# Output projection of an attention and LSTM kernel: one float32 matmul replaced by three float16 ones, with high and low parts made by three engines

## The chip, the cores and the metric

The kernel runs on one core of a Trainium2 chip. The metric is the device time of one execution, in microseconds. A core has TensorE (PE, matmuls; its weight loads are listed as PEld), VectorE (DVE), ScalarE (ACT), GpSimd (POOL) and SyncE (SP), whose queue issues most of the DMAs.

## The reference, cut to what matters

```python
x = x + attn(layernorm(x))          # x: 32 batches x 256 rows x 128
x = x + lstm(layernorm(x))          # 32 steps, one per batch
# attn: h = rms_norm(x); q, k, v = split(h @ w_qkv.T); rope(q), rope(k)
#       16 heads of 64; 4 extra keys and values in front; causal softmax
#       out = softmax(q k^T / 8) v   (256 x 1024 per batch)
#       return out @ w_out.T         # the output projection, 1024 -> 128
```

## The kernel before

Five instruction streams are written out by hand, one per engine; each engine works in order, and semaphores tie the engines together. The streams run over iterations j = 0 to 34 and in each over eight slots s = 0 to 7, one for each pair of heads. In an iteration, batch j is projected to queries and keys and rotated (slot s handles pair s), batch j-1 goes through scores, exponentials and values, batch j-2 is normalised and put through the output projection, and batch j-3 does its step of the LSTM (called gates and state). So four batches are in flight, and a full iteration is 8 slots of PE work.

The path that the prediction follows, for one iteration:

- `invert(j-2)` on DVE at the end of slot 1 takes the reciprocal of the softmax sums of batch j-2 (line 832, tile `linv`).
- SP stores it to DRAM (`store_linv`, line 301) and then spreads it over the partitions into `rinv` (`spread_linv`, line 312, four DMAs of 256 KB). Its place in SP's queue is slot 2, after `swap(j, 2)` and so ahead of `swap(j, 3)`.
- `swap(j, s)` (line 294) moves the partition-swapped half of the rotation, `rope_b` to `rope_c`. `rotate(j, s)` on DVE (lines 798 and 799) writes `rope_a` and `rope_b`; since `rope_b` has two buffers, `rotate(j, 5)` waits until the swap of pair 3 has landed. `rope_add` on POOL (line 407) adds the two to `qk`, and ACT's `hi` (line 529) makes the float16 copy `qk_h`.
- `divide` on DVE (line 845) multiplies two pairs of `raw`, the attention output of batch j-2, by `rinv`: parts n = 0 and 1 in slot 4, n = 2 and 3 in slot 5. A part n holds the pairs 2n and 2n+1.
- `project_out` on PE (line 1179) multiplies a part with `wo_sb` in float32, four matmuls of 128x128x128 per part; parts 0 and 1 in slot 5, parts 2 and 3 in slot 6. A float32 matmul shows as two instructions in the profile.
- `residual` (line 850) and `second_stats` on DVE in slot 6, `rstd` on POOL and `second_norm` on ACT in slot 7, `transpose_xn` and the gates on PE in slots 0 to 2 of the next iteration.

Between these stand, in each slot, `project` (line 1034) at the slot's start on PE, `scores_for_max` (line 1073), `scores_t` (line 1098) and `attend` (line 1142), in some slots `values` (lines 1053 and 1056) and `sums` (line 1163); on DVE `rotate` and four `maxima` (line 809); on POOL `prob_add` (line 400); on ACT `exp`, `raw_copy` and `hi`. In slots 3 and 7 PE begins with `transpose_top` (line 1081), which waits for all `maxima` of four pairs. `h_low` on DVE (line 742) in slot 5 makes the low part of the next batch's input. `project(s)` waits until DVE has read the bank of `project(s-1)`.

The other projections are already done in two float16 parts each: `SPLIT` lists the three products high x high, high x low, low x high.

## Time and profile before

| | us |
|---|---|
| median of 3 runs | 1133.13 |
| lowest and highest of them | 1126.74 to 1135.27 |
| profiled execution, its own time | 1133.03 |
| span of its trace | 1131.2 |

The span runs from the first to the last instruction in the trace; the time of the profiled execution is 1.8 us longer. An iteration shows in the trace as the distance of one `linv` instruction to the next. In the rows, a time in brackets at the end is how long the engine sat idle before the instruction, and what released it.

### The profile page before, as it was taken

To read this page: it belongs to the slowest core of one execution; us is meant where nothing else is said; L and a number is where in the kernel's file an instruction comes from. 1 tells how busy PE (TensorE), PEld (TensorE's weight loads), DVE (VectorE), ACT (ScalarE), POOL (GpSimd) and SP (SyncE) were. 2 spreads that over 40 slices of the span, in tenths; PEclk is the share of its full clock that TensorE was granted. 3 is DMA by queue.
4 is the path that set the end of the run, shared out by engine and by line. 5 is a ranking of instruction groups with operands and counts; after the bars stand their busy time and mean duration, and the time that the engine had idled before them with its cause. 6 is when DMAs were issued, how large, how long until landed. Compare 5 with 4: busy or idle time off the path is not lost.

```text
span 1131.2 us, 47261 instructions
## 1 busy us (share of the span) xinstructions
PE 1080.3 (95%) x18443; PEld 813.6 (72%) x18443; DVE 930.0 (82%) x3305; ACT 698.4 (62%) x1575; POOL 634.8 (56%) x816
## 2 busy tenths in 40 slices
...
DMA packets 78031, 120.52 MB, mean 107 GB/s; under 512 B 13041, under 2 KB 35954, under 8 KB 77682
## 3 DMA queue, kind: packets, MB, share of 16 engines
...
## 4 chain that ended last, share of the span: by engine, by line
PE 59%; DVE 16%; DMA 14%; SPq 4%; issue 3%; POOL 2%; ACT 1%; DVEq 0%; POOLq 0%
PE bank_pv L1142 11%; PE bank L1034 11%; DMA rope_c<-rope_b 10%; PE bank_st L1098 8%; PE bank_sum L1179 5%; PE bank_sum L1163 4%; DVE masked L809 4%; PE bank_sm L1073 4%; PE bank L1056 3%; DMA linv_scratch<-linv 3%; SPq L312 3%; DVE linv L832 2%; DVE rope_a L798 2%; PE bank L1281 2%; PE bank L1283 2%
## 5 line engine op out<-in xcount | busy, mean ns | idle before, releaser
L407 POOL TENSOR_TENSOR qk<-rope_a,rope_c 128x512 f32<-128x512 f32 x256 | 341.0, 1332 | 312.9 <-DMA rope_c<-rope_b 288.9
L809 DVE CUSTOM_DVE_ANT_0 masked<-bank_sm,mask_q 128x132 bf16<-128x132 f32 (+1 forms) x1024 | 307.1, 355 | 17.7 <-PE bank_sm L1073 17.2
L798 DVE TENSOR_TENSOR rope_a<-bank,cos 128x512 f32<-128x512 f32 x256 | 174.1, 680 | 130.1 <-PE bank L1034 83.7
L400 POOL TENSOR_TENSOR prob<-prob 128x264 f32<-128x264 f32 x256 | 210.8, 823 | 117.1 <-ACT prob L544 108.3
L529 ACT ACTIVATE qk_h<-qk 128x512 f16<-128x512 f32 x256 | 160.4, 627 | 172.2 <-POOL qk L407 171.7
L544 ACT ACTIVATE prob<-bank_st 128x784 f32<-128x784 f32 x256 | 209.3, 817 | 59.7 <-PE bank_st L1107 58.9
L1142 PE MATMUL bank_pv<-prob,v_sb 128*64 128x256 f32 (+1 forms) x2048 | 224.8, 340 | 0.6 <-DVE raw L825 0.6
L1098 PE MATMUL bank_st<-qk 64*64 64x256 f32 (+3 forms) x4096 | 186.3, 299 | 0.4 <-issue 0.2
L1098 PEld LDWEIGHTS bank_st<-qk 64*64 64x64 f32 x4096 | 167.7, 134 | 9.6 <-issue 1.3
L799 DVE TENSOR_TENSOR rope_b<-bank,sin 128x512 f32<-128x512 f32 x256 | 173.8, 679 | 0.0
L1142 PEld LDWEIGHTS bank_pv<-prob,v_sb 128*64 128x64 f32 x2048 | 124.3, 136 | 54.4 <-issue 0.9
L1034 PE MATMUL bank<-h_hi,w_hi 128*128 128x256 f16 x512 | 143.5, 280 | 5.8 <-DVE rope_b L799 5.0
L1034 PE MATMUL bank<-h_hi,w_lo 128*128 128x256 f16 x512 | 141.8, 277 | 0.0
L1034 PE MATMUL bank<-h_lo,w_hi 128*128 128x256 f16 x512 | 141.6, 277 | 0.0
L1179 PE MATMUL bank_sum<-wo_sb,raw 128*128 128x128 f32 x992 | 122.7, 276 | 0.0
L1179 PEld LDWEIGHTS bank_sum<-wo_sb,raw 128*128 128x128 f32 x992 | 116.0, 192 | 1.9 <-DVE raw L845 1.1
L578 ACT ACTIVATE v_sb<-bank 128x512 f32<-128x512 f32 x128 | 75.8, 593 | 48.2 <-PE bank L1053 28.7
L569 ACT ACTIVATE raw<-bank_pv 128x256 f32<-128x256 f32 x256 | 97.7, 382 | 4.1 <-PE bank_pv L1148 3.1
L845 DVE SCALAR_TENSOR_TENSOR raw<-rinv,raw 128x512 f32<-128x512 f32 x124 | 96.6, 819 | 2.0 <-DMA rinv<-linv_scratch 1.8
L1073 PEld LDWEIGHTS bank_sm<-qk_h 64*64 64x64 f16 x2048 | 37.6, 105 | 82.7 <-issue 56.6
L1073 PE MATMUL bank_sm<-qk_h 64*64 64x68 f16 (+3 forms) x2048 | 86.7, 246 | 4.4 <-ACT qk_h L529 3.1
L809 DVE DVE_READ_ACCUMULATOR2_ANT top<- 128x1 bf16 x1024 | 85.7, 84 | 0.1
...
## 6 DMA issues: line engine op xcount, KB each, us to landing
rope_c<-rope_b SPq DMA_DIRECT2D x512, 128.0 KB, 2.3
...
v_end<-v_end_scratch SPq DMA_DIRECT2D x64, 8.0 KB
v_sb<-pm_v SPq DMA_DIRECT2D x63, 8.0 KB
```

Of the source, the lines that this page charges most:

```text
L400: G.tensor_tensor(prob_2[:, s % 4, :, :], prob[:, s % 4, :, 0:NT - Q1], prob[:, s % 4, :, C0 + Q1:SCOL], ALU.add).then_inc(S["prob_added"], 1)
L407: G.tensor_tensor(qk[:, s, :].rearrange("p (u n) -> p u n", u=2)[:, :, 0:NT], rope_a[:, (NPAIR * j + s) % 3, :].rearrange("p (u n) -> p u ...
L529: A.activation(qk_h[:, s, :].rearrange("p (u n) -> p u n", u=2)[:, :, 0:NT], qk[:, s, :].rearrange("p (u n) -> p u n", u=2)[:, :, 0:NT], A ...
L544: A.activation(prob[:, s % 4, :, :], ps_st[:, :, 0:SCOL], ACT.Exp).then_inc(S["exp_done"], 1)
L798: V.tensor_tensor(rope_a[:, (NPAIR * j + s) % 3, :], proj_bank(j, s)[:, :], cos[:, :], ALU.mult)
L799: V.tensor_tensor(rope_b[:, s % 2, :], proj_bank(j, s)[:, :], sin[:, :], ALU.mult).then_inc(S["qk_read"], 1)
L809: ins = V.tensor_tensor_reduce(masked[:, e, c0:c0 + n], ps_sm[:, e, c0:c0 + n], mask_q[:, c0:c0 + n], 1.0, LOWEST, ALU.add, ALU.max, top[: ...
L1034: last = T.matmul(proj_bank(j, s)[:, u * NT:(u + 1) * NT], W[q][:, col:col + P], H[p][:, par, NPM:NKEY], start=(i == 0), stop=(i == 2))
L1073: last = T.matmul(ps_sm[OWN[SIDE[qb]], e, c0:c0 + n], qk_h[OWN[e], s, qb * HB:qb * HB + HB], qk_h[OWN[e], s, NT:NT + n], start=True, stop= ...
L1098: T.matmul(ps_st[OWN[SIDE[kb]], e, st_cols(blk)], qk[OWN[e], s, NT + kb * HB:NT + kb * HB + HB], qk[OWN[e], s, q0:NT], start=(kc == 0), st ...
L1142: last = T.matmul(ps_pv[OWN[e], q0:NT], v_sb[:, kc, col:col + DH], prob[:, s % 4, e, c0:c0 + NT - q0], start=(kc == 0), stop=(kc == 1))
L1179: last = T.matmul(y_out(cj)[:, q * D:(q + 1) * D], raw[:, par, s, q * P:(q + 1) * P], wo_sb[:, s, :], start=(alone and s == 0 and q == 0), ...
```

## The change

The output projection is done as the others are. `w_out` is loaded into a raw area and cast to `wo_hi` and `wo_lo` (scale 64, once, at the start; `residual` divides by 64 again). For each part, ACT casts the normalised `raw` to float16 (`y_high`, into `y_hl`), and the difference is the low part (`y_low`): parts 0 and 2 (pairs 0, 1, 4, 5) by DVE (`y_low_dve`), parts 1 and 3 by POOL. PE does three float16 matmuls for each float32 one. The last two batches are split otherwise: the last but one gets all its low parts from POOL, the last from DVE.

`y_hl` lies in the same memory as `rinv`, so a `rinv` of the next batch may be loaded only when the projection is done (`spread_linv` waits for `y_ready`). In the engines' orders, `project_out` of parts 0 and 1 moves from slot 5 to slot 6, parts 2 and 3 go from the front of slot 6 to its end; `residual` and `second_stats` move to slot 7, `rstd` behind a `rope_add`, `second_norm` to slot 0 of the next iteration, `xt_high` and `xt_low` to slot 1; `transpose_xn` and the gates go to the end of their slots on PE, and ACT's `gate_tanh` one slot later.

```diff
@@ -77,12 +77,14 @@
+        o_raw = pre_f[:, 3 * DI + 8 * P + NCONST:3 * DI + 8 * P + NCONST + DI]
...
-        wo_sb = sb("wo_sb", [P, NPAIR, D], f32)
+        wo_hi = sb("wo_hi", [P, NPAIR, D], f16)
+        wo_lo = sb("wo_lo", [P, NPAIR, D], f16)
@@ -138,7 +140,8 @@
-        rinv = sb("rinv", [P, NPAIR, NT], f32)
+        y_hl = sb("y_hl", [P, 4, 2, 2 * NT], f16)
+        rinv = y_hl[:, :, :, :].rearrange("p n u m -> p (n u m)").bitcast(f32).rearrange("p (s n) -> p s n", s=NPAIR)
@@ -304,7 +306,7 @@
-                wait(sp, S["norm_done"], 4 * cj)
+                wait(sp, S["y_ready"], cj)
@@ -409,6 +411,13 @@
+            def y_low(cj, par, n):
+
+                pool.wait_ge(S["y_hi_done"], 4 * cj + n + 1)
+                done = S["y_lo_pool" if cj < NB - 2 else "y_lo_done"]
+                G.tensor_tensor(y_hl[:, n, 1, :].rearrange("p (s n) -> p s n", s=2), raw[:, par, 2 * n:2 * n + 2, :],
+                                y_hl[:, n, 0, :].rearrange("p (s n) -> p s n", s=2), ALU.subtract).then_inc(done, 1)
+
             def rstd(cj):
@@ -432,14 +441,21 @@
-                    if c and s == 7 and j < NB:
-                        rstd(j - 2)
+                    if s == 6 and c and j < NB:
+                        y_low(j - 2, p, 3)
...
+                    if s == 5 and c and j < NB:
+                        y_low(j - 2, p, 1)
+                    if s == 7 and c and j < NB:
+                        rstd(j - 2)
...
+                    if s in (5, 6) and j == NB:
+                        y_low(j - 2, p, 2 * (s - 5))
+                        y_low(j - 2, p, 2 * (s - 5) + 1)
@@ -514,6 +531,8 @@
+                act.wait_ge(S["ld_wo"], 16)
+                cast(A.activation(wo_hi[:, :, :].rearrange("p c d -> p (c d)"), o_raw, ACT.Copy, scale=WS))
@@ -630,6 +649,12 @@
+            def y_high(cj, par, n):
+
+                act.wait_ge(S["norm_done"], 4 * cj + n + 1)
+                A.activation(y_hl[:, n, 0, :].rearrange("p (s n) -> p s n", s=2), raw[:, par, 2 * n:2 * n + 2, :],
+                             ACT.Copy).then_inc(S["y_hi_done"], 1)
+
@@ -638,18 +663,21 @@
-                    if s == 3 and b:
-                        copy_top(j - 1, 1)
...
-                    if s == 0 and d and j != NB + 1:
+                    if s == (0 if j > NB else 1) and d and j != NB + 1:
...
+                    if s == 1 and j == NB + 1:
+                        for n in range(4):
+                            y_high(j - 2, p, n)
...
-                    elif s in (1, 2) and d and j - 3 < NB - 1:
-                        gate_tanh(j - 3, s - 1)
+                    elif s in (2, 3) and d and j - 3 < NB - 1:
+                        gate_tanh(j - 3, s - 2)
+                    if s == 3 and b:
+                        copy_top(j - 1, 1)
@@ -657,14 +685,17 @@
+                    if s == 5 and c and j <= NB:
+                        y_high(j - 2, p, 0)
+                        y_high(j - 2, p, 1)
...
-                    if s == 7 and c and j < NB:
-                        second_norm(j - 2)
+                    if s == 0 and d and j <= NB:
+                        second_norm(j - 3)
@@ -689,6 +720,9 @@
+                    if s == 5 and c and j <= NB:
+                        y_high(j - 2, p, 2)
+                        y_high(j - 2, p, 3)
@@ -780,11 +814,14 @@
+                V.scalar_tensor_tensor(wo_lo[:, :, :].rearrange("p c d -> p (c d)"), o_raw, WS,
+                                       wo_hi[:, :, :].rearrange("p c d -> p (c d)"), ALU.mult,
@@ -844,10 +881,17 @@
+            def y_low_dve(cj, par, n):
+
+                dve.wait_ge(S["y_hi_done"], 4 * cj + n + 1)
+                V.tensor_tensor(y_hl[:, n, 1, :].rearrange("p (s n) -> p s n", s=2), raw[:, par, 2 * n:2 * n + 2, :],
+                                y_hl[:, n, 0, :].rearrange("p (s n) -> p s n", s=2), ALU.subtract).then_inc(S["y_lo_done"], 1)
+
...
-                V.tensor_tensor(at3(x_sb, cj), y_out(cj), at3(x_sb, cj), ALU.add).then_inc(S["x1_done"], 1)
+                V.scalar_tensor_tensor(at3(x_sb, cj), y_out(cj), 1.0 / WS, at3(x_sb, cj), ALU.mult,
+                                       ALU.add).then_inc(S["x1_done"], 1)
@@ -912,11 +956,13 @@
+                    if s == 7 and c and j < NB:
+                        residual(j - 2)
...
-                    if s == 0 and d and j != NB + 1:
+                    if s == (0 if j > NB else 1) and d and j != NB + 1:
@@ -924,9 +970,13 @@
+                    if s == 5 and c and j < NB:
+                        y_low_dve(j - 2, p, 0)
...
-                    if s == 6 and c:
+                    if s == 6 and c and j < NB:
+                        y_low_dve(j - 2, p, 2)
+                    if s == 6 and c and j >= NB:
@@ -941,6 +991,9 @@
+                            if i > 0:
+                                y_low_dve(j - 2, p, i - 1)
+                        y_low_dve(j - 2, p, 3)
@@ -952,7 +1005,7 @@
-                    if s == 6 and c:
+                    if s == (6 if j >= NB else 7) and c:
@@ -1172,13 +1225,20 @@
-                pe.wait_ge(S["norm_done"], 4 * cj + n + 1)
+                if cj < NB - 2:
+                    pe.wait_ge(S["y_lo_pool" if n % 2 else "y_lo_done"], 2 * cj + n // 2 + 1)
+                else:
+                    pe.wait_ge(S["y_lo_done"], 2 * (NB - 2) + 4 * (cj - NB + 2) + n + 1)
+                if cj == 0 and n == 0:
+                    pe.wait_ge(S["casts_dve"], 7)
...
-                        last = T.matmul(y_out(cj)[:, q * D:(q + 1) * D], raw[:, par, s, q * P:(q + 1) * P], wo_sb[:, s, :],
-                                        start=(alone and s == 0 and q == 0), stop=(s == NPAIR - 1 and q == QT - 1),
-                                        skip_group_check=True)
+                        at = s % 2 * NT + q * P
+                        for i, (u, v) in enumerate(SPLIT):
+                            last = T.matmul(y_out(cj)[:, q * D:(q + 1) * D], y_hl[:, n, u, at:at + P], WO[v][:, s, :],
+                                            start=(alone and s == 0 and q == 0 and i == 0),
+                                            stop=(s == NPAIR - 1 and q == QT - 1 and i == 2), skip_group_check=True)
@@ -1308,10 +1368,6 @@
-                    elif s == 0 and d and j <= NB:
-                        transpose_xn(j, j - 3)
-                    if s in (1, 2) and d and j <= NB:
-                        gates(j, j - 3, s - 1)
@@ -1327,7 +1383,10 @@
-                    if s in (5, 6) and c and j != NB:
+                    if s == 6 and c and j < NB:
+                        project_out(j - 2, p, 0)
+                        project_out(j - 2, p, 1)
+                    if s in (5, 6) and j == NB + 1:
@@ -1354,10 +1413,15 @@
+                    if s == 6 and c and j < NB:
+                        project_out(j - 2, p, 2)
+                        project_out(j - 2, p, 3)
...
-                if isinstance(j, int) and j == 2:
-                    pe.wait_ge(S["casts_dve"], 6)
+                    if s == 0 and d and j <= NB:
+                        transpose_xn(j, j - 3)
+                    if s in (1, 2) and d and j <= NB:
+                        gates(j, j - 3, s - 1)
```

GpSimd's queue from slot 4 to slot 7 of one iteration. The line with `qk` is `rope_add` (L407 before, L409 after), the one with `prob` is `prob_add`; the first row of each piece is the `rope_add` of pair 3. Before:

```order
L407 TENSOR_TENSOR qk<-rope_a,rope_c 128x2x256 [waits swapped1,st_ready]
L400 TENSOR_TENSOR prob<-prob 128x264 [waits exp_done,sum_ready]
L407 TENSOR_TENSOR qk<-rope_a,rope_c 128x2x256 [waits swapped0,st_ready]
L400 TENSOR_TENSOR prob<-prob 128x264 [waits exp_done,sum_ready]
L407 TENSOR_TENSOR qk<-rope_a,rope_c 128x2x256 [waits swapped1,st_ready]
```

After:

```order
L409 TENSOR_TENSOR qk<-rope_a,rope_c 128x2x256 [waits swapped1,st_ready]
L402 TENSOR_TENSOR prob<-prob 128x264 [waits exp_done,sum_ready]
L409 TENSOR_TENSOR qk<-rope_a,rope_c 128x2x256 [waits swapped0,st_ready]
L418 TENSOR_TENSOR y_hl<-raw,y_hl 128x512 [waits y_hi_done]
L402 TENSOR_TENSOR prob<-prob 128x264 [waits exp_done,sum_ready]
L418 TENSOR_TENSOR y_hl<-raw,y_hl 128x512 [waits y_hi_done]
L409 TENSOR_TENSOR qk<-rope_a,rope_c 128x2x256 [waits swapped1,st_ready]
```

The low part of part 1 stands behind the `rope_add` of pairs 3 and 4, that of part 3 ahead of the `rope_add` of pair 5.

PE's queue in slot 6, from its `project` on (L1034 before, L1088 after). Before:

```order
L1034 MATMUL bank<-h_lo,w_hi 128x256
L1179 MATMUL bank_sum<-wo_sb,raw 128x128 [waits norm_done]
L1179 MATMUL bank_sum<-wo_sb,raw 128x128 x3
...
L1053 MATMUL bank<-w_hi,h_hi 128x512 [waits h_lo_done]
...
L1073 MATMUL bank_sm<-qk_h 64x68 [waits max_done,hi_done]
...
L1081 MATMUL bank_sm<-ident_b,top 128x128 [waits max_done]
```

After:

```order
L1088 MATMUL bank<-h_lo,w_hi 128x256
L1239 MATMUL bank_sum<-wo_hi,y_hl 128x128 [waits y_lo_done]
...
L1239 MATMUL bank_sum<-wo_hi,y_hl 128x128 [waits y_lo_pool]
...
L1107 MATMUL bank<-w_hi,h_hi 128x512 [waits h_lo_done]
...
L1127 MATMUL bank_sm<-qk_h 64x68 [waits max_done,hi_done]
...
L1239 MATMUL bank_sum<-wo_hi,y_hl 128x128 [waits y_lo_done]
...
L1135 MATMUL bank_sm<-ident_b,top 128x128 [waits max_done]
```

Parts 0 and 1 now stand ahead of `values`, parts 2 and 3 at the end of the slot, and the second and fourth part wait for GpSimd (`y_lo_pool`).

DVE's queue from slot 5 to slot 6, without the `maxima` rows. Before:

```order
L799 TENSOR_TENSOR rope_b<-bank,sin 128x512
L845 SCALAR_TENSOR_TENSOR raw<-rinv,raw 128x512 [waits spread1]
L845 SCALAR_TENSOR_TENSOR raw<-rinv,raw 128x512
L742 SCALAR_TENSOR_TENSOR h_lo<-bank,nw,h_hi 128x256 [waits h_hi_done]
...
L798 TENSOR_TENSOR rope_a<-bank,cos 128x512 [waits swapped0,rope_sum,qk_proj]
...
L850 TENSOR_TENSOR x_sb<-bank_sum,x_sb 128x256 [waits y_ready]
```

After (`raw<-y_hl,raw` is `divide`, since `rinv` is a view of `y_hl`):

```order
L836 TENSOR_TENSOR rope_b<-bank,sin 128x512
L882 SCALAR_TENSOR_TENSOR raw<-y_hl,raw 128x512 [waits spread1]
L882 SCALAR_TENSOR_TENSOR raw<-y_hl,raw 128x512
L887 TENSOR_TENSOR y_hl<-raw,y_hl 128x512 [waits y_hi_done]
L776 SCALAR_TENSOR_TENSOR h_lo<-bank,nw,h_hi 128x256 [waits h_hi_done]
...
L835 TENSOR_TENSOR rope_a<-bank,cos 128x512 [waits swapped0,rope_sum,qk_proj]
...
L887 TENSOR_TENSOR y_hl<-raw,y_hl 128x512 [waits y_hi_done]
```

One low part comes in behind the divisions of slot 5, one behind the rotation of slot 6, and `residual` leaves slot 6.

## Rows read from the trace of the kernel before

**Rows 1.** The page's head and its first part: busy time of each engine.

```profile
span 1131.2 us, 47261 instructions
PE 1080.3 (95%) x18443; PEld 813.6 (72%) x18443; DVE 930.0 (82%) x3305; ACT 698.4 (62%) x1575; POOL 634.8 (56%) x816
```

**Rows 2.** Stretches: length, busy us of PE, PEld, DVE, ACT, POOL; clock; DMA share, GB/s.

```profile
413.60:446.20 32.60, 30.74 (x540) 23.24 (x538) 27.19 (x94) 19.02 (x43) 17.79 (x22) 1.00 0.36 101
```

**Rows 3.** Timeline of DVE: start, length, line, what; several iterations.

```profile
80.30 1.75 DVE L832 RECIPROCAL linv<-bank_sum 128x256 f32<-128x256 f32 x1
...
408.79 1.75 DVE L832 RECIPROCAL linv<-bank_sum 128x256 f32<-128x256 f32 x1
...
424.91 0.69 DVE L798 TENSOR_TENSOR rope_a<-bank,cos 128x512 f32<-128x512 f32 x1 [2.98 <-DMA rope_c<-rope_b]
...
443.76 1.75 DVE L832 RECIPROCAL linv<-bank_sum 128x256 f32<-128x256 f32 x1
...
509.08 1.75 DVE L832 RECIPROCAL linv<-bank_sum 128x256 f32<-128x256 f32 x1
...
519.91 1.29 DVE L845 SCALAR_TENSOR_TENSOR raw<-rinv,raw 128x512 f32<-128x512 f32 x2
...
522.77 0.69 DVE L798 TENSOR_TENSOR rope_a<-bank,cos 128x512 f32<-128x512 f32 x1 [1.24 <-DMA rope_c<-rope_b]
...
523.98 1.84 DVE L845 SCALAR_TENSOR_TENSOR raw<-rinv,raw 128x512 f32<-128x512 f32 x2
525.74 0.47 DVE L742 SCALAR_TENSOR_TENSOR h_lo<-bank,nw,h_hi 128x256 f16<-128x256 f32 x1
...
540.50 0.30 DVE L809 CUSTOM_DVE_ANT_0 masked<-bank_sm,mask_q 128x132 bf16<-128x132 f32 x1 [0.36 <-PE bank_sm L1073]
...
541.63 1.75 DVE L832 RECIPROCAL linv<-bank_sum 128x256 f32<-128x256 f32 x1
...
1037.35 1.75 DVE L832 RECIPROCAL linv<-bank_sum 128x256 f32<-128x256 f32 x1
```

**Rows 4.** Timeline of SP: the spreading of `rinv`, and the swap of pair 3 behind it.

```profile
513.70 2.40 SPq L312 DMA_DIRECT2D rinv<-linv_scratch  x4
516.28 2.19 SPq L294 DMA_DIRECT2D rope_c<-rope_b  x2
```

**Rows 5.** Timeline of PE, slots 5 and 6 of the same iteration.

```profile
520.57 0.28 PE L1034 MATMUL bank<-h_hi,w_hi 128*128 128x256 f16 x1
...
521.45 1.95 PE L1179 MATMUL bank_sum<-wo_sb,raw 128*128 128x128 f32 x16
...
525.16 0.28 PE L1034 MATMUL bank<-h_hi,w_hi 128*128 128x256 f16 x1
...
525.83 1.95 PE L1179 MATMUL bank_sum<-wo_sb,raw 128*128 128x128 f32 x16
527.62 0.38 PE L1053 MATMUL bank<-w_hi,h_hi 128*128 128x512 f16 x1
...
530.18 0.28 PE L1081 MATMUL bank_sm<-ident_b,top 128*128 128x128 bf16 x2
```

**Rows 6.** Timeline of PE near the end: float16 matmuls 128x128, back to back.

```profile
1100.17 0.22 PE L1241 MATMUL bank_st<-f_hi,xt 128*128 128x128 f16 x1
...
1100.84 0.22 PE L1241 MATMUL bank_sm<-f_hi,xt 128*128 128x128 f16 x1
```

**Rows 7.** Timeline of POOL, slots 4 and 5 of the same iteration.

```profile
522.78 1.27 POOL L407 TENSOR_TENSOR qk<-rope_a,rope_c 128x512 f32<-128x512 f32 x1 [4.95 <-DMA rope_c<-rope_b]
524.02 1.25 POOL L400 TENSOR_TENSOR prob<-prob 128x264 f32<-128x264 f32 x1
525.23 1.71 POOL L407 TENSOR_TENSOR qk<-rope_a,rope_c 128x512 f32<-128x512 f32 x1
```

**Rows 8.** Timeline of ACT in slot 4, the copy of pair 3.

```profile
524.09 0.63 ACT L529 ACTIVATE qk_h<-qk 128x512 f16<-128x512 f32 x1 [3.48 <-POOL qk L407]
```

**Rows 9.** Waits of DVE over the span: us in total, times, longest.

```profile
DVE rope_a L798 <- DMA rope_c<-rope_b: 43.6, 31, 3.1
```

More of the change, by code:

```diff
@@ L172, in build @@
             "qk_proj qk_read swapped0 swapped1 rope_sum hi_done sm_ready max_done top_tr top_copied "
-            "st_ready exp_done prob_added pv_ready raw_done sum_ready linv_done linv_stored spread0 spread1 norm_done y_ready x1_done "
+            "st_ready exp_done prob_added pv_ready raw_done sum_ready linv_done linv_stored spread0 spread1 norm_done y_hi_done y_lo_done y_lo_pool y_ready x1_done "
             "v_ready v_done v_end sx_done sx_rstd xn_ready xt_ready xt_hi_done xt_lo_done gate_ready gate_read c_hi_done state_done "
```

13 lines of the change are left out of this document (7 added, 6 removed).

## The prediction

> **What bounds the kernel now.** Start with the page's busy times [rows 1]: TensorE is busy 95% of 1131.2 us, VectorE 82%, GpSimd 56%. That invites the reading "TensorE is the bound, a cheaper projection is a gain". It is half true. The next view is VectorE's timeline at the one instruction that stands once in each iteration, the reciprocal `linv` [rows 3]. From 509.08 to 541.63 an iteration takes 32.55 us, from 408.79 to 443.76 it takes 34.97 us with the same instructions. In the second one TensorE is busy 30.74 of 32.60 us, at the full granted clock of 1.00 [rows 2], so it waited. The first and the last of the 30 starts of full iterations (80.30 and 1037.35) give a mean of 957.05/29 = 33.00 us.
>
> What differs is a transfer. Behind `linv` SP stores it, spreads it (2.40 us of issue) and only then issues the swap of pair 3 [rows 4]. VectorE's `rotate` of slot 5 waits for that swap to land. This moment, called L below, is the start of that rope_a row. L is 522.77 - 509.08 = 13.69 us behind `linv` in the short iteration and 424.91 - 408.79 = 16.12 us in the long one. From L to the next `linv` it is 541.63 - 522.77 = 18.86 and 443.76 - 424.91 = 18.85 us [rows 3]. So two things end together: TensorE's own work, 32.55 us, and a loop through the DMAs, (time from `linv` to L) + 18.86. The loop has no slack left: each 0.1 us put between L and the next `linv` lengthens the iteration by about 0.1 us. The mean L is then 33.00 - 18.86 = 14.14 us behind `linv`. VectorE waited at this point 31 times, 43.6 us in all [rows 9]; here 1.24 us.
>
> The question for the change is therefore not what TensorE saves but what it puts behind L.
>
> **What TensorE saves.** Two parts in float32 take 527.62 - 525.83 = 1.79 us [rows 5]. Twelve float16 matmuls of 128x128 take 1100.84 - 1100.17 = 0.67 us, 56 ns each [rows 6]; the form of the operands is the same. A part now has 2 x 2 x 3 = 12, so two parts take 1.34 us. Saved: 0.45 us for two parts, 0.90 us for a batch, 28.8 us for 32 batches if nothing waits.
>
> **What stands between L and the end of slot 6 before.** Slot 7 begins with the `transpose_top` at 530.18, which is L + 7.41 [rows 5]. VectorE's rotation takes 1.21 us (522.77 to 523.98), the two divisions 1.76 (to 525.74) [rows 3], and TensorE reaches parts 2 and 3 at 525.83 [rows 5], 0.1 us later.
>
> **What stands there after.** Part by part, with L = 0:
>
> GpSimd: `rope_add` of pair 3 at 0.0, `prob_add` at 1.25, `rope_add` of pair 4 at 2.46, done at 526.94, which is 4.17 [rows 7]. These three were there before, but nobody on TensorE waited for them so soon. Now the low part of part 1 is queued behind them, though its data could be had earlier. Its price is not in the trace (float16 in and out). The nearest row is the `rope_add` with the same 128x512 elements and two inputs: 1.27 us alone, 1.71 us when VectorE's divisions run beside it [rows 7]. The upper bound is 1.9 us, the crowded one and a little for the conversion. From below I take 0.7, less than any row of half the size. I take 1.3, the lone one, since VectorE then reads PSUM in `h_low` and the maxima. The low part of part 0 on VectorE starts at 525.74, or 2.97, beside the `rope_add`, which I let lengthen by 0.2. Part 1 is ready at 4.17 + 0.2 + 1.3 = 5.7 (5.1 to 6.3).
>
> This crowding is a row: two divisions take 1.29 us at 519.91, with GpSimd idle, and 1.84 us at 523.98 with it busy [rows 3, 7]. The Trainium skill says so too (GPSIMD Engine Reference, Specifications): GpSimd's SBUF interface is shared with VectorE, and instructions of VectorE with two SBUF inputs contend. By that rule both new kinds of instruction crowd each other, and the trace agrees.
>
> The same page (Performance versus the Vector engine) speaks against the division of labour itself: elementwise work with two inputs costs GpSimd about 2.6 cycles an element, roughly double VectorE, and belongs on VectorE. By its figure the low part would be an estimate of 512 x 2.6 / 1.2 GHz = 1.1 us, which would make the sum 6 us smaller.
>
> ACT: its copy of pair 3 begins at 524.09 and takes 0.63 us [rows 8]. The high parts 0 and 1 are queued behind it, at 0.6 us each: done by L + 3.2. That is ahead of GpSimd's 4.4 and near VectorE's 2.97, so they decide nothing. The exponential of slot 5 is 1.2 us later; TensorE needs it only behind `values`.
>
> TensorE: the projection of slot 6 waits for the rotation, till 1.2, and ends at 1.9. Part 0 waits for VectorE's low part (2.97 + 0.6 to 0.9, so till 3.8) and ends at 4.5. Part 1 waits till 5.7 and ends at 6.4. `values`, scores and `attend` take 530.18 - 527.62 = 2.56 us [rows 5], to 8.95; the low parts of 2 and 3 are there by then (GpSimd: 5.7 + 0.8 + 1.3 to 1.7, so 8.2 at the latest). Parts 2 and 3 take 1.34 us: slot 7 begins at L + 10.3.
>
> That is 10.3 - 7.4 = 2.9 us later than before, with TensorE idle for about 3.9 us in slot 6.
>
> From slot 7 to the next `linv` I count no change. `residual` and `second_stats` (some 1.2 us of VectorE) come into slot 7, but VectorE has waited by then. The gates' move takes away a wait of 0.36 us ahead of the maxima of slot 1 (the row at 540.50 [rows 3]), and `xt_low` comes into the same slot at about the same price. The new wait of SP, `y_ready` of the batch before, was met an iteration's third earlier. Behind it stand `rinv`, all swaps, and so the rotations; it would matter only if the projection ran past slot 2. From `linv` to L I keep 14.14 us: the same queue, the same bytes.
>
> **The sum.** Iteration: 14.14 + 18.86 + 2.9 = 35.9 us, against 33.0. It holds in the 30 iterations in which the projection stands behind a swap: 30 x 2.9 = 87 us. The last two batches have no swaps; there the chain division, high part, low part is longer by a low part of 1.3 us on GpSimd and some 1.6 us at the very end, less 2 x 0.9 us in TensorE, and the start gets one more cast each on ACT and VectorE of about 1.2 us: together +3 us, an estimate. Span 1131.2 + 87 + 3 = 1221; the profiled execution was 1.8 us longer than its span, 1133.03, and the median 1133.13 is the same within 0.1. Forecast 1223 us. With the bounds of GpSimd's low part (-0.6 to +0.6 us, 30 times) it is 1205 to 1241.
>
> **Rivals.**
>
> *TensorE alone decides (faster).* If the swap landed early enough, or the low parts were ready when TensorE comes, the 28.8 us would be saved, less 3: 1107 us. For it: TensorE's 32.55 us is a floor hit in many iterations. Against: the 18.86 us repeat to 0.01 us in iterations 2.4 us apart in length. Even this needs L at least 2 us earlier. Chance 0.06.
>
> *Unchanged (within 1%).* GpSimd's part is hidden, so that an iteration loses 1.6 us as in the next rival, and L comes 1.3 to 1.9 us earlier because the transfers collide less: 1133 + 3 + 30 x (-0.3 to +0.3), 1127 to 1145 us. The spread of L, 13.69 to 16.12, shows that it moves by such amounts; against it, 13.69 would have to become 12.4 at the most. Chance 0.06.
>
> *VectorE's chain decides, not GpSimd (slower, less).* The place is slot 6, with GpSimd's low part ready before VectorE's. Then part 0 starts at 3.8, both end at 5.1, slot 7 begins at 5.1 + 2.56 + 1.34 = 9.0: +1.6 us an iteration, 1133 + 48 + 3 = 1184 us. It decides if the low part on GpSimd is done by 4.5; its queue is busy till 4.17, so that needs an operation of 0.3 us. A milder form is a GpSimd queue that drains faster once the longer iteration sets it free. Chance 0.15.
>
> *The wait grows past TensorE (slower, more).* The exponential of slot 5, 1.2 us later, and `rope_add` of pair 5 behind both low parts, could delay slots 6 to 0: another 0.5 to 1 us each time, 1240 to 1255 us. Chance 0.13.
>
> My case, GpSimd's low part of part 1 as the last to arrive: chance 0.60.
>
> A measurement of this kernel can tell about 1% from no change. Slower by over 1%: 0.60 + 0.15 + 0.13 = 0.88; within 1%: 0.06; faster: 0.06. The range, 8 in 10, takes in half of the milder rival and part of the heavier: 1178 to 1245 us.
>
> **What would show it.** Right: `linv` to `linv` near 35.9 us, L to the next `linv` near 21.8, a wait of TensorE in front of the projection that names GpSimd's `y_hl`, near 1.3 us each time, and one that names VectorE's, near 1.9; TensorE's busy share near 87%; the matmuls of a part 0.67 us. Wrong in size: GpSimd's `y_hl` far from 1.3 us, or L not 14.1 us behind `linv`. Wrong in mechanism: iterations below 33 us, or TensorE waiting elsewhere, at `transpose_top` or the exponential.

## The result, and the profile after

| | before | after |
|---|---|---|
| time, median | 1133.04 us (4 runs) | 1253.79 us (4 runs; 1253.48 to 1256.66) |
| ratio | | 1.108 (95%: 1.103 to 1.113) |
| profiled span | 1131.2 us | 1252.3 us |
| mean iteration, first to 30th `linv` | 33.00 us | 36.92 us |
| mean L, counted from `linv` | 14.15 us | 14.02 us |
| L to the next `linv` | 18.69 to 19.71 us, mean 18.85 | 21.72 to 23.34 us, mean 23.10 |

The last two rows are of the iterations in which VectorE waits for the swap: all 29 before, 21 of 29 after. Slower, as forecast, but by 120.8 us and not by 90; 1253.79 lies above the range's end of 1245. An iteration grew by 3.92 us instead of 2.9.

The page's head and its first part after the change, against [rows 1]:

```profile
span 1252.3 us, 48543 instructions
PE 1099.5 (88%) x18955; PEld 807.2 (64%) x18955; DVE 1015.7 (81%) x3370; ACT 760.8 (61%) x1704; POOL 723.9 (58%) x880
```

TensorE's projection got cheaper, and yet its busy time rose from 1080.3 to 1099.5 us. Work that costs less and sums to more is the first hint at what the forecast lacked: the same matmuls ran slower somewhere. VectorE's busy time rose by 86 us, though its 64 low parts would take 64 x 0.68 = 44 us at their shortest length.

Waits of TensorE over the span (us in total, times, longest):

```profile
PE bank_sum L1239 <- DVE y_hl L887: 76.6, 30, 3.1
PE bank_pv L1195 <- DVE raw L862: 16.5, 30, 0.6
PE bank L1088 <- DVE rope_b L836: 11.8, 20, 1.9
...
PE bank_sum L1239 <- POOL y_hl L418: 3.1, 18, 0.2
```

The place is the forecast one, in front of the projection. But the long wait is for VectorE's low part of part 0 (2.5 us each), and GpSimd's part 1 adds 0.2. The second row is new too: in slot 1 of the next iteration `attend` waits 0.55 us each time for VectorE's copy of `raw`; before, such waits sum to 0.6 us.

Two neighbouring iterations, VectorE's timeline. The rows are the reciprocals and the two rotations at L:

```profile
635.55 1.75 DVE L869 RECIPROCAL linv<-bank_sum 128x256 f32<-128x256 f32 x1
...
649.05 0.69 DVE L835 TENSOR_TENSOR rope_a<-bank,cos 128x512 f32<-128x512 f32 x1 [0.27 <-DMA rope_c<-rope_b]
...
672.35 1.75 DVE L869 RECIPROCAL linv<-bank_sum 128x256 f32<-128x256 f32 x1
...
685.71 0.69 DVE L835 TENSOR_TENSOR rope_a<-bank,cos 128x512 f32<-128x512 f32 x1 [0.47 <-DMA rope_c<-rope_b]
...
707.43 1.75 DVE L869 RECIPROCAL linv<-bank_sum 128x256 f32<-128x256 f32 x1
```

From L to the next `linv` the first takes 672.35 - 649.05 = 23.30 us, the second 707.43 - 685.71 = 21.72. The forecast was 18.86 + 2.9 = 21.76. The second is the forecast iteration; 24 of 29 are like the first.

TensorE's timeline tells the two apart. First iteration, then second:

```profile
653.82 0.23 PE L1239 MATMUL bank_sum<-wo_hi,y_hl 128*128 128x128 f16 x1 [2.51 <-DVE y_hl L887]
...
654.84 0.23 PE L1239 MATMUL bank_sum<-wo_hi,y_hl 128*128 128x128 f16 x1 [0.17 <-POOL y_hl L418]
...
655.53 0.63 PE L1107 MATMUL bank<-w_hi,h_hi 128*128 128x512 f16 x1
...
657.22 1.30 PE L1151 MATMUL bank_st<-qk 64*64 64x256 f32 x16
...
661.02 0.28 PE L1135 MATMUL bank_sm<-ident_b,top 128*128 128x128 bf16 x2
...
690.49 0.23 PE L1239 MATMUL bank_sum<-wo_hi,y_hl 128*128 128x128 f16 x1 [2.38 <-DVE y_hl L887]
...
692.18 0.38 PE L1107 MATMUL bank<-w_hi,h_hi 128*128 128x512 f16 x1
...
693.09 0.72 PE L1151 MATMUL bank_st<-qk 64*64 64x256 f32 x16
...
696.10 0.28 PE L1135 MATMUL bank_sm<-ident_b,top 128*128 128x128 bf16 x2
```

The projection's matmuls are alike, and the waits nearly (2.51 and 2.38 us). But the first `values` matmul lasts 0.63 us in one and 0.38 in the other, the scores 1.30 and 0.72. Slot 7 begins at L + 11.97 in the first and at L + 10.39 in the second; the forecast was 10.3. Stretches of 2 us, columns as in [rows 2], first iteration and then second:

```profile
652.00:654.00 2.00, 0.18 (x3) 0.18 (x4) 2.00 (x3) 2.00 (x6) 2.00 (x2) 1.00 0.21 75
654.00:656.00 2.00, 1.83 (x26) 1.38 (x24) 2.00 (x11) 1.25 (x3) 2.00 (x3) 0.88 0.01 4
656.00:658.00 2.00, 2.00 (x21) 1.06 (x23) 1.51 (x5) 0.60 (x1) 2.00 (x2) 0.50 0.09 34
658.00:660.00 2.00, 2.00 (x38) 1.53 (x31) 1.37 (x8) 1.04 (x2) 0.37 (x2) 0.77 0.32 110
...
690.00:692.00 2.00, 1.34 (x21) 1.18 (x22) 2.00 (x11) 1.91 (x5) 2.00 (x2) 1.00 0.03 8
692.00:694.00 2.00, 2.00 (x48) 1.35 (x45) 2.00 (x6) 0.60 (x1) 2.00 (x3) 1.00 0.00 0
```

Behind an idle stretch of 2.5 us the granted clock falls from 1.00 to 0.50, from 2.4 to 1.2 GHz, while TensorE has work, and comes back some 3.4 us later. What is lost is (0.12 + 0.50 + 0.23) x 2 = 1.7 us of TensorE's time; slot 7 shows 1.58 us of it. In the second iteration the clock stayed, behind 2.38 us. Over the trace, the five iterations that keep the full clock have idle stretches of 2.02 to 2.38 us in front of the projection, and of the 24 in which it falls 23 have 2.51 us or more; but one of them has 2.21 us, so the length of this stretch does not decide alone.

Last, why VectorE's low part came late. Timelines of VectorE and of GpSimd, same slot:

```profile
650.26 1.83 DVE L882 SCALAR_TENSOR_TENSOR raw<-y_hl,raw 128x512 f32<-128x512 f32 x2
652.02 1.75 DVE L887 TENSOR_TENSOR y_hl<-raw,y_hl 128x512 f16<-128x512 f32 x1
...
656.41 0.75 DVE L887 TENSOR_TENSOR y_hl<-raw,y_hl 128x512 f16<-128x512 f32 x1
```

```profile
651.51 1.71 POOL L409 TENSOR_TENSOR qk<-rope_a,rope_c 128x512 f32<-128x512 f32 x1
653.18 1.61 POOL L418 TENSOR_TENSOR y_hl<-raw,y_hl 128x512 f16<-128x512 f32 x1
...
655.45 1.15 POOL L418 TENSOR_TENSOR y_hl<-raw,y_hl 128x512 f16<-128x512 f32 x1
```

The low part (L887) begins beside GpSimd's `rope_add` and lasts 1.75 us. It ends at 653.77, 0.55 us behind the `rope_add`'s end of 653.22: it seems to have done its work only then. Of the 64 low parts of VectorE 34 last 0.68 to 0.75 us and 26 last 1.75; only four lie between.

### The profile page after: what moved, and what is told of

It is laid out like the page before. It is cut to its first block, busy times and chain, and to the rows that moved or that the text cites. A ratio compares the mean times of both kernels' runs of the same rounds, so it can differ in the third digit from the quotient of the medians.

```text
span 1252.3 us, 48543 instructions
## 1 busy us (share of the span) xinstructions
PE 1099.5 (88%) x18955; PEld 807.2 (64%) x18955; DVE 1015.7 (81%) x3370; ACT 760.8 (61%) x1704; POOL 723.9 (58%) x880
## 4 chain that ended last, share of the span: by engine, by line
PE 38%; DMA 19%; DVE 18%; POOL 9%; SPq 7%; issue 6%; ACT 1%; DVEq 0%; POOLq 0%; ACTq 0%
DMA rope_c<-rope_b 13%; PE bank_sum L1239 8%; PE bank_pv L1195 6%; DMA linv_scratch<-linv 6%; PE bank L1088 5%; SPq L314 5%; POOL qk L409 4%; PE bank_st L1151 4%; DVE linv L869 4%; DVE masked L846 3%; PE bank L1107 3%; PE bank_sum L1216 3%; POOL y_hl L418 3%; PE bank_sm L1127 2%; PE bank L1110 2%
## 5 line engine op out<-in xcount | busy, mean ns | idle before, releaser
L409 POOL TENSOR_TENSOR qk<-rope_a,rope_c 128x512 f32<-128x512 f32 x256 | 351.3, 1372 | 263.8 <-DMA rope_c<-rope_b 254.1
L846 DVE CUSTOM_DVE_ANT_0 masked<-bank_sm,mask_q 128x132 bf16<-128x132 f32 (+1 forms) x1024 | 307.0, 355 | 25.3 <-PE bank_sm L1127 25.2
L1195 PE MATMUL bank_pv<-prob,v_sb 128*64 128x256 f32 (+1 forms) x2048 | 224.7, 340 | 19.0 <-DVE raw L862 16.5
L1151 PE MATMUL bank_st<-qk 64*64 64x256 f32 (+3 forms) x4096 | 190.8, 304 | 1.1 <-ACT prob L563 1.1
L1239 PE MATMUL bank_sum<-wo_hi,y_hl 128*128 128x128 f16 x992 | 114.4, 240 | 79.8 <-DVE y_hl L887 76.6
L1151 PEld LDWEIGHTS bank_st<-qk 64*64 64x64 f32 x4096 | 172.6, 138 | 11.0 <-ACT prob L563 1.5
L1195 PEld LDWEIGHTS bank_pv<-prob,v_sb 128*64 128x64 f32 x2048 | 127.5, 136 | 72.3 <-issue 23.8
L1088 PE MATMUL bank<-h_hi,w_hi 128*128 128x256 f16 x512 | 142.9, 279 | 12.9 <-DVE rope_b L836 11.8
L1239 PEld LDWEIGHTS bank_sum<-wo_hi,y_hl 128*128 128x128 f16 x992 | 87.8, 108 | 97.4 <-DVE y_hl L887 85.0
L1088 PE MATMUL bank<-h_hi,w_lo 128*128 128x256 f16 x512 | 141.9, 277 | 0.0
L1088 PE MATMUL bank<-h_lo,w_hi 128*128 128x256 f16 x512 | 141.5, 276 | 0.0
L1239 PE MATMUL bank_sum<-wo_lo,y_hl 128*128 128x128 f16 x496 | 102.2, 240 | 0.0
L882 DVE SCALAR_TENSOR_TENSOR raw<-y_hl,raw 128x512 f32<-128x512 f32 x124 | 101.7, 860 | 0.3 <-DMA y_hl<-linv_scratch 0.3
```

The lines of the kernel that those rows point to most:

```text
L409: G.tensor_tensor(qk[:, s, :].rearrange("p (u n) -> p u n", u=2)[:, :, 0:NT], rope_a[:, (NPAIR * j + s) % 3, :].rearrange("p (u n) -> p u ...
L846: ins = V.tensor_tensor_reduce(masked[:, e, c0:c0 + n], ps_sm[:, e, c0:c0 + n], mask_q[:, c0:c0 + n], 1.0, LOWEST, ALU.add, ALU.max, top[: ...
L1088: last = T.matmul(proj_bank(j, s)[:, u * NT:(u + 1) * NT], W[q][:, col:col + P], H[p][:, par, NPM:NKEY], start=(i == 0), stop=(i == 2))
L1151: T.matmul(ps_st[OWN[SIDE[kb]], e, st_cols(blk)], qk[OWN[e], s, NT + kb * HB:NT + kb * HB + HB], qk[OWN[e], s, q0:NT], start=(kc == 0), st ...
L1195: last = T.matmul(ps_pv[OWN[e], q0:NT], v_sb[:, kc, col:col + DH], prob[:, s % 4, e, c0:c0 + NT - q0], start=(kc == 0), stop=(kc == 1))
L1239: last = T.matmul(y_out(cj)[:, q * D:(q + 1) * D], y_hl[:, n, u, at:at + P], WO[v][:, s, :], start=(alone and s == 0 and q == 0 and i == 0 ...
```

## The experiments

The theory after the two traces had three terms on top of [rows 3]'s 18.86 us: the moved projection, the wait for the parts, and the fall of the clock. The rivals said that the loop through L explains less than that, and that the part instructions cost whatever their place. All ratios are to the kernel before, measured beside each run.

### Keep TensorE busy while it waits

40 float16 matmuls of zeros are added to the projection's accumulation in front of the first wait, so the result is the same.

```
+    if cj < NB - 2 and n == 0:
+        for _ in range(40):
+            T.matmul(y_out(cj)[:, 0:P], w_hi[:, 0:P], zz[:, :], start=False, stop=False, ...)
     if cj < NB - 2:
         pe.wait_ge(S["y_lo_pool" if n % 2 else "y_lo_done"], 2 * cj + n // 2 + 1)
```

> The changed kernel with 40 float16 matmuls of 128x128 with a zero operand put ahead of the wait for the first low part in slot 6 (40 x 56 ns = 2.24 us, inside the wait of 2.5 to 2.6 us). Theory 'the clock is the missing term' (L to the next linv is 21.7 us in the iterations at clock 1.00 and 23.0 to 23.3 us in those at 0.95): granted clock 1.00 everywhere, L to linv 21.6 to 22.0 us in all iterations, time 1253.8 - 30 x 1.25 = 1216 us (1208 to 1226). Rival 'the low part on VectorE, 1.75 us instead of the 0.6 to 0.9 forecast, lengthens the loop': the filled wait changes nothing, 1250 to 1260 us. If the filler runs past the wait, iterations get longer than after.

Measured: 1213.0 us (1212.1 to 1213.9), ratio 1.072 (1.067 to 1.077), as expected. In the 13 iterations of 29 in which VectorE waits for the swap it is now 21.72 to 21.74 us from L to `linv`; the mean iteration is 35.47 us, the clock 1.00 in all 29, and the span's clock 0.988 instead of 0.955. Rows of one iteration, and its stretch behind the projection:

```profile
346.94 0.23 PE L1244 MATMUL bank_sum<-wo_hi,y_hl 128*128 128x128 f16 x1 [0.37 <-DVE y_hl L889]
...
348.64 0.38 PE L1109 MATMUL bank<-w_hi,h_hi 128*128 128x512 f16 x1
```

```profile
348.00:350.00 2.00, 2.00 (x37) 1.43 (x40) 2.00 (x7) 0.87 (x3) 2.00 (x3) 1.00 0.00 0
```

1200 matmuls more make the kernel 41 us faster, though VectorE's low part still ends at the same place behind L. That is the clock's term, shown: it is what the forecast lacked.

The other 16 iterations do not hang on L: the swap has landed, or all but landed, when VectorE comes to the rotation. In nine of them that costs nothing (34.86 to 35.09 us). In six the landing is so early that GpSimd's `rope_add` starts beside the state's instruction `c`, which then lasts 1.49 us instead of 0.42; these six take 36.07 us.

### The new order with the old projection

The changed kernel's order with float32 weights and matmuls from `raw`, and no high and low parts.

```
-    for i, (u, v) in enumerate(SPLIT):
-        last = T.matmul(..., y_hl[:, n, u, at:at + P], WO[v][:, s, :], ...)
+    last = T.matmul(..., raw[:, par, s, q * P:(q + 1) * P], wo_sb[:, s, :], ...)
```

> The changed kernel's order of work with the old float32 projection straight from raw: no high or low parts at all. Theory (loop through the DMAs): the order alone puts 1.2 + 0.67 + 1.79 + 2.56 + 1.79 = 8.05 us between L and slot 7 against 7.41 before, so 33.6 us an iteration, 1133 + 30 x 0.64 = 1152 us (1145 to 1160), no wait of TensorE at the projection, clock 1.00. Rival 'the moved order is the cause, not the parts': above 1200 us. Rival 'TensorE's own work decides': 1133 us.

Measured: 1157.9 us, ratio 1.024 (1.020 to 1.028), within the range expected. From L to `linv` it is 19.75 us, 0.9 more than the mean before, and TensorE waits at no projection. The ten shortest iterations take 33.17 us, 0.62 more than TensorE's own 32.55 before; 0.55 us is the wait at `attend`, which this run has too (16.5 us in all). The iterations give the decomposition: before 33.00, new order 33.82, with the parts and a full clock 35.47, with the clock's fall 36.92. Order 0.8, parts 1.65, clock 1.45 us; times 30 it is 25, 50 and 44 us. About 0.1 us of the order's 0.8 is one iteration of 37.01 us, in which the clock fell behind another idle stretch, of 2.14 us in front of `project`.

### All low parts on VectorE

```
-    pool: y_low(j - 2, p, 1) in slot 5, y_low(j - 2, p, 3) in slot 6
+    dve:  y_low_dve(j - 2, p, 1) in slot 5, y_low_dve(j - 2, p, 3) in slot 6
```

> The changed kernel with all four low parts by VectorE (part 1 in slot 5, part 3 in slot 6), none by GpSimd. Theory (VectorE's instruction with two inputs and GpSimd's instructions exclude each other, so that work moved from one to the other still queues): low part 0 ends at L + 4.75 us as now, low part 1 at about L + 6.05 instead of 5.8, slot 7 0.3 to 0.9 us later, 1265 us (1250 to 1285). Rival (GpSimd's own slower low parts, 1.2 to 1.6 us against 0.7 on VectorE, hold up the projection): faster by 30 us or more, 1225 or less.

Measured: 1254.6 us, ratio 1.110 (1.107 to 1.114), the changed kernel's time, and within the range expected. TensorE starts part 0 at L + 4.77 in every iteration in which VectorE waits for the swap, part 1 at L + 5.92 to 6.03. So taking the subtraction from GpSimd gains nothing: GpSimd's slower instruction, which the forecast took for the last to arrive, is not the cause. VectorE's own timeline of this run:

```profile
611.91 1.83 DVE L878 SCALAR_TENSOR_TENSOR raw<-y_hl,raw 128x512 f32<-128x512 f32 x2
613.66 2.90 DVE L883 TENSOR_TENSOR y_hl<-raw,y_hl 128x512 f16<-128x512 f32 x2
```

Two low parts take 2.90 us, where two alone take 1.3. This run also has an iteration that keeps the full clock behind an idle stretch as long as those behind which it falls:

```profile
988.27 0.23 PE L1234 MATMUL bank_sum<-wo_hi,y_hl 128*128 128x128 f16 x1 [2.59 <-DVE y_hl L883]
```

```profile
990.00:992.00 2.00, 1.88 (x44) 1.24 (x41) 2.00 (x8) 0.60 (x1) 0.50 (x1) 1.00 0.00 0
```

### What VectorE and GpSimd do to each other, by itself

Six phases behind the last store of the kernel before, on scratch tiles of 128x512 float32: 8 instructions of VectorE, 5 of GpSimd, each phase begun together. In the first two one of the engines does only 128x8 copies.

```
+    dve:  (0, 2, 5) tensor_tensor(sbuf, sbuf)   (3) tensor_tensor(psum, sbuf)   (4) tensor_copy(sbuf)
+    pool: (1, 2, 3, 4) tensor_tensor(sbuf, sbuf)   (5) tensor_copy(sbuf)
```

> The kernel before with six phases appended behind the last store, on scratch tiles, 128x512 float32 each: (0) 8 VectorE additions of two SBUF tiles alone, (1) 5 GpSimd additions alone, (2) both together, (3) VectorE's with one input from PSUM beside GpSimd's, (4) VectorE copies (one SBUF input) beside GpSimd's additions, (5) VectorE's additions of two SBUF tiles beside GpSimd copies. Exclusion theory: alone 0.6 us and 1.25 us an instruction; in phase 2 an instruction of VectorE ends about 0.55 us behind one of GpSimd's, so 1.7 to 1.9 us while GpSimd runs, and GpSimd's grow too; in phase 3 both keep their lengths. Phases 4 and 5 tell which inputs matter; by the float32 copies and conversions seen beside GpSimd so far I expect no loss in 4 and a loss in 5. Rival (a shared bandwidth, both slowed in proportion): in phase 2 VectorE about 0.9 us each, evenly.

Measured, timeline of VectorE, then of GpSimd (rows of one kind are grouped, the length is from the first's start to the last's end):

```profile
1129.44 4.91 DVE L1009 TENSOR_TENSOR raw<-rope_a 128x512 f32<-128x512 f32 x8 [5.13 <-DMA out<-x_sb]
...
1140.75 10.23 DVE L1009 TENSOR_TENSOR raw<-rope_a 128x512 f32<-128x512 f32 x8 [1.28 <-POOL qk L457]
1151.11 4.88 DVE L1011 TENSOR_TENSOR raw<-bank_pv,rope_a 128x512 f32<-128x512 f32 x8
1157.36 8.10 DVE L1013 COPY raw<-rope_a 128x512 f32<-128x512 f32 x8 [1.37 <-POOL qk L457]
1165.59 7.00 DVE L1009 TENSOR_TENSOR raw<-rope_a 128x512 f32<-128x512 f32 x8
```

```profile
1134.49 6.17 POOL L457 TENSOR_TENSOR qk<-rope_b 128x512 f32<-128x512 f32 x5 [1.90 <-DVE raw L1009]
1140.83 8.40 POOL L457 TENSOR_TENSOR qk<-rope_b 128x512 f32<-128x512 f32 x5 [0.17 <-POOL qk L457]
1151.11 6.16 POOL L457 TENSOR_TENSOR qk<-rope_b 128x512 f32<-128x512 f32 x5 [1.89 <-DVE raw L1009]
1157.44 7.07 POOL L457 TENSOR_TENSOR qk<-rope_b 128x512 f32<-128x512 f32 x5 [0.17 <-POOL qk L457]
1165.58 4.67 POOL L459 COPY qk<-rope_b 128x512 f32<-128x512 f32 x5 [1.08 <-DVE raw L1013]
```

Alone, 4.91 and 6.17 us; together 10.23, almost the sum of 11.08. Within it VectorE's instructions last 1.74 us each while GpSimd works, against 0.68 behind it and 0.69 alone, as in the kernel; GpSimd's last 1.70 us, against 1.26. With one input from PSUM (1151.11) neither loses anything. The rival, a shared bandwidth that slows all evenly, would give VectorE a single length. I missed phase 4: a plain float32 copy of one SBUF tile and GpSimd's addition exclude each other too, 1.48 us a piece against 0.41 behind it. The Trainium skill has both (SBUF — State Buffer, "SBUF: two separate sides"): the port pair that VectorE and GpSimd share is an exclusive lock for a whole instruction, taken by an instruction of GpSimd, or by one of VectorE with two SBUF inputs or in a two-port mode, and a float32 copy within SBUF is its example of that mode. The runs agree on which instructions block; the lengths are from the runs.

### Move the parts ahead of L

High parts 0 and 1 in slot 4 in front of pair 3's copy, low part 0 at the end of slot 4, low part 1 in front of GpSimd's `rope_add(3)`, high parts 2 and 3 in slot 5.

```
 act   y_high(0), y_high(1): s == 5 -> s == 4     y_high(2), y_high(3): ahead of hi() in s == 5
 dve   y_low_dve(0): s == 5 -> end of s == 4
 pool  y_low(1): ahead of rope_add(3)             y_low(3): behind rope_add(4)
```

> The changed kernel with the high and low parts 0 and 1 taken ahead of the landing of pair 3's swap (high parts 0, 1 by ScalarE in slot 4, low part 0 by VectorE at the end of slot 4, low part 1 by GpSimd ahead of rope_add(3)), high parts 2, 3 in slot 5 ahead of hi(4), low part 3 behind rope_add(4). Loop theory (the loss is the loop from the landing of pair 3's swap through division, high part, low part, projection, top of slot 7, back to the reciprocal): what follows that landing shrinks from 11.7 us to about 8.6 us, the period from 36.9 to about 33.9 us, TensorE's idle time at the projection becomes too short for its clock to fall, and the time is about 1160 us (1150 to 1180). Rival (the 16 high and low part instructions of an iteration cost what they cost on VectorE, GpSimd and ScalarE wherever they stand): 1230 us or more.

Measured: 1178.9 us, ratio 1.044 (1.041 to 1.046), within the range expected; 19 of 29 iterations take 34.35 to 34.38 us (mean 34.38), against 33.9 expected. This takes back 75 of the 121 us with the same instructions, so place decides and the second theory falls. Some 41 of the 75 us are the clock's, as in the run with filler: it stays at 1.00 in all 29 iterations here. What bounds it now is VectorE:

```profile
747.34 0.69 DVE L887 TENSOR_TENSOR y_hl<-raw,y_hl 128x512 f16<-128x512 f32 x1
747.94 0.69 DVE L835 TENSOR_TENSOR rope_a<-bank,cos 128x512 f32<-128x512 f32 x1
748.54 0.68 DVE L836 TENSOR_TENSOR rope_b<-bank,sin 128x512 f32<-128x512 f32 x1
749.14 2.84 DVE L882 SCALAR_TENSOR_TENSOR raw<-y_hl,raw 128x512 f32<-128x512 f32 x2
```

The rotation at 747.94 waits for no swap, as in most iterations of this run. Divisions 2 and 3 take 2.84 us beside GpSimd, against 1.29 for 0 and 1. In each stretch of 2 us from 740 to 760 VectorE is busy for 2.00, so its own chain is the bound here, and TensorE waits 0.97 us for its `h_low`, 0.39 for its maxima and 0.34 for its low part 2.

### All divisions and high parts ahead of L

As above, and divisions 2 and 3 in slot 4, all high parts in slot 4, half of the projection at the end of slot 5.

```
-    if s == 5 and c and j - 2 < NB - 1:   (dve)
-        divide(j - 2, p, 2); divide(j - 2, p, 3)
+        y_low_dve(j - 2, p, 0); divide(j - 2, p, 2); divide(j - 2, p, 3)      (dve, s == 4)
```

> The order of the early run, and also: divisions 2, 3 in slot 4, in the time in which VectorE waits for pair 3's swap, all four high parts in slot 4, the projection's halves at the ends of slots 5 and 6 instead of both in slot 6. Theory (loop from that landing): what follows the landing is about 6.5 us, the loop's period about 31.9 us, near TensorE's own busy time of an iteration of about 31.6 us, so about 1100 us (1095 to 1125), faster than the kernel before. Rival (VectorE's and GpSimd's mutual exclusion gives it back, as with the spread in halves): 1133 us or more.

Measured: 1205.3 us, ratio 1.067 (1.064 to 1.069). A clear miss: 34.62 us or more an iteration instead of 31.9, 26 us slower than the milder version. The state's instruction `c` now fell beside a `rope_add`, and the rotation of slot 5 behind it. TensorE's `project` of slot 6 waits for that rotation, some 2.1 us in most iterations:

```profile
PE bank L1087 <- DVE rope_b L836: 63.3, 34, 2.4
```

In eight of 29 iterations the clock falls behind this wait, and they take 36.0 to 36.7 us; those at full clock take 34.62 to 35.38. Timeline of VectorE in this run, and then in the next:

```profile
623.23 1.49 DVE L948 SCALAR_TENSOR_TENSOR c<-ga,gb 128x256 f32<-128x256 f32 x1
...
628.56 0.68 DVE L887 TENSOR_TENSOR y_hl<-raw,y_hl 128x512 f16<-128x512 f32 x1
```

### The same, with c ahead of the divisions

```
+    if s == 4 and d and j != NB + 1: state(j - 3, 1)        # now ahead of divide(0..3)
```

> The same move of c in the run that has all four divisions, all high parts and low part 0 in slot 4 (1205 us, iteration 34.6 us, VectorE without a pause between slots 3 and 7). Theory (VectorE's own chain there, in which two-input instructions queue with GpSimd's, sets the iteration): c 0.35 instead of 1.4 us, iteration 33.6 us, 1172 us (1160 to 1185), still slower than the kernel before. Rival (the projection or the landing of the swaps sets it): 1205 us, no change.

Measured: 1214.6 us, ratio 1.075 (1.072 to 1.078): slower still.

```profile
698.79 0.42 DVE L948 SCALAR_TENSOR_TENSOR c<-ga,gb 128x256 f32<-128x256 f32 x1
...
708.28 1.75 DVE L887 TENSOR_TENSOR y_hl<-raw,y_hl 128x512 f16<-128x512 f32 x1
```

`c` fell from 1.49 to 0.42 us as expected, and slot 5's rotation came 1.07 us earlier. But low part 2 in slot 6 began 0.07 us behind a `rope_add` of GpSimd instead of 0.21 us ahead of one, and went from 0.68 to 1.75 us. What was gained in slot 4 was lost in slot 6, 1.07 us each, and TensorE got a wait for that low part (25.3 us in all). The mean iteration went from 35.1 to 35.6 us. TensorE's one wait of 2.06 us became four, 0.91, 0.65, 0.39 and 0.88 us, for the rotation, `h_low`, the maxima and low part 2: most iterations went from 34.63 to 35.58 us. None of the four is long, and the clock falls in no iteration of this run, which gives a part back.

### The kernel before, with earlier divisions

Divisions 2 and 3 in slot 4, alone, and then with `c` ahead of them.

```
-    if s == 5: divide(j - 2, p, 2); divide(j - 2, p, 3)
+    if s == 4: divide(0), divide(1), divide(2), divide(3)
```

> The kernel before with divisions 2 and 3 moved from slot 5 to slot 4, nothing else. Loop theory: 2.6 us leave the stretch behind the landing of pair 3's swap, the iteration falls from 33.0 to TensorE's own 32.5 us: 1120 us (1116 to 1126). Rival (the loop is given back in slot 4, as in the run with the spread in halves): 1133 us, no change.

> The run with divisions 2, 3 in slot 4 (kernel before), and the state's instruction c moved ahead of the four divisions. In that run c stood behind them, beside GpSimd's rope_add, and lasted 1.4 us instead of 0.35, and slot 5's rotation waited behind it. Theory (VectorE's order in slot 4, through the mutual exclusion with GpSimd, is what took the gain): slot 5's rotation starts about 1 us earlier, at 14.4 us after the reciprocal, the iteration is 32.6 us, TensorE's own, and the time 1122 us (1116 to 1134). Rival (another cause): 1144 us as there.

Measured: 1144.4 us, ratio 1.012 (1.009 to 1.015), and with `c` ahead 1128.9 us, ratio 0.999 (0.997 to 1.000). The first missed in its sign: `c` took 0.96 to 1.50 us beside GpSimd in 17 of 29 iterations, and TensorE waited for the rotation behind it (21.6 us in all, against 5.0 before); once, behind 2.18 us, the clock fell (37.05 us). The second confirms that reason, since moving one instruction gave 15 us back; and 16 of its 29 iterations stand at TensorE's 32.55 us (mean 32.76), in the range expected. It is no faster than before within what was measured, so there is no new best kernel here.

### The spreading of 1/l in two halves around pair 3's swap

So that the swap lands earlier, in the changed kernel and in the one before:

```
-    if c and s == 2 and j - 2 < NB - 1: spread_linv(j - 2)
+    if c and s in (2, 3) and j - 2 < NB - 1: spread_linv(j - 2, s - 2)
```

> The changed kernel with the spreading of rinv cut in two: the half for parts 0 and 1 ahead of the swap of pair 3, the other half behind it. Theory (everything hangs on L): L comes 1.5 to 2.5 us earlier, iterations are shorter by 1 to 2 us (the divisions of parts 2 and 3 may then wait for their half), 1253.8 - 30 to 60 = 1194 to 1224 us. Rival 'the parts chain alone makes the iteration, L does not matter': 1250 to 1257 us.

> The kernel before with the same cut of the spreading. Theory: TensorE's own 32.55 us and the loop (L + 18.86) tie, so an earlier L only removes the excess of the mean over 32.55: 30 x 0.45 = 13 us, 1120 us (1116 to 1125), every iteration at 32.55. Rival 'the loop decides alone': as in the other kernel, 30 to 60 us less. Rival 'L is no bound': 1133 us, or more if the divisions come to wait.

Measured: 1273.3 us, ratio 1.125 (1.120 to 1.130), and 1134.9 us, ratio 1.002 (1.000 to 1.005). In both the theory missed. The swap did land earlier: GpSimd's `rope_add` began 9.8 to 13.2 us behind `linv`, instead of 12.4 to 16.4, and VectorE hardly waited for it any more. But in most iterations GpSimd's work then ran beside divisions 0 and 1, which took 1.8 to 2.8 us instead of 1.29, or beside `c`. In the changed kernel TensorE's idle stretch in front of the projection grew with it, to 2.7 us or more in most iterations, and the clock fell in 27 of 29. An earlier landing helps only as far as VectorE is done with its two-input work.

## Why the prediction was right or wrong

**The loop through L: right, with a stretch mis-sized by 0.17 us.** L itself stayed: 14.02 us for 14.14. The 18.86 us that "repeat to 0.01 us" are a chance of the two rows chosen. Of the 19 iterations longer than 32.6 us, 15 have 18.69 or 18.70 us from L to the next `linv`; that is the loop's own stretch. At TensorE's 32.55 us it is anything from 18.75 to 19.71 us, because L comes early and there is slack. At full clock the changed kernels repeat it to some hundredths where VectorE waits (19.75 to 19.79 with the old projection, 21.72 to 21.74 with filler). And not every iteration hangs on L: with the filler 16 of 29 do not.

**The 2.9 us behind L: right as a sum.** At full clock it is 21.72 us for 21.76, slot 7 at L + 10.39 for 10.3; against the loop's own 18.69 it is 3.03 us. At full clock the mean iteration is 35.47 us for 35.9 and the time 1213 us for 1223: the forecast without its missing term was 10 us high.

**Its parts: one mis-sized, hidden by the other.** VectorE's low part of part 0 was put at 0.6 to 0.9 us, TensorE's start at 3.8; it took 1.75 us and started at 4.77. GpSimd's of part 1 was put at 1.3 us with the end at 5.7; it took 1.61 us and TensorE started at 5.79. GpSimd remains the last by a little, so the sum holds, and that is luck: TensorE's two waits were put at 1.9 and 1.3 us and are 2.5 and 0.2. But "GpSimd's low part as the last to arrive" is no cause, since the run without it has the same time. The rule on the shared interface was quoted, and then 0.2 us were charged for a conflict that costs VectorE up to one GpSimd instruction. [Rows 3, 7] had shown 1.29 against 1.84 us for two divisions: they end at 525.82, 0.55 us behind the end of GpSimd's `prob_add` at 525.27, as the low part ends 0.55 us behind a `rope_add` now.

**"With TensorE idle for about 3.9 us": the step that failed.** The idle time was counted as a wait and nothing else, on the strength of the full clock in [rows 2], where TensorE also waited. There it waited less at a time: the longest wait of that iteration is 1.32 us, and of all full iterations 1.48. Now one stretch of 2.0 to 3.1 us, mostly 2.5 to 2.6, stands in front of the projection, the clock falls to 1.2 GHz behind it in 24 of 29 iterations, and the loop, which has no slack in this stretch, takes nearly all of it: 1.37 us more behind L on average (23.10 for 21.73). The forecast had put this term at nothing; taking it away with the filler gives back 41 us.

**"From slot 7 to the next `linv` I count no change": right.** 707.43 - 696.10 = 11.33 us for 541.63 - 530.18 = 11.45 before [rows 3, 5]. The wait for `rope_b` grows from 5.0 to 11.8 us; it is the one for the rotation at L itself, which the forecast's path holds already. The wait of 0.55 us at `attend` stands in this stretch and was not forecast; the stretch is no longer for it.

**Start and end, +3 us: right.** 1131.2 + 30 x 3.92 = 1248.8, against a span of 1252.3, leaves 3.5 us for all that lies outside.

**The rivals.** "The wait grows past TensorE" gave 1240 to 1255 us, which holds the time, but by late exponentials and `rope_add`, of which the trace shows no growing wait of TensorE: right number, wrong mechanism. "TensorE alone decides" did not come near even with the parts moved ahead of L, because VectorE then fills its own slots 3 to 6. "VectorE's chain decides" is what the run with early parts became (1178.9 us for 1184), by another way than its text.

**Open.** What decides, beside the length of the idle stretch, whether the clock falls: it fell behind 2.14 and 2.21 us and stayed behind 2.59 and, in the changed kernel with the spreading in halves, once behind 3.00. And how to bring the version with everything ahead of L below 34.6 us; that VectorE has hardly a pause there and TensorE waits for it is seen, what would free it was not tried.
